# Repeated multiplications of a constant matrix on TensorE, in six places of a four-layer convolution kernel

## The reference, cut to what matters

```python
x = x + _L0_conv_ref(_gn(x), ...)   # 1x1 conv, norm, SiLU, 6 gated radial bases, 1x1 conv, norm, SiLU
x = x + _L1_conv_ref(_gn(x), ...)   # projection, depthwise 3x3 conv, SiLU, linear attention, layer norm, projection
x = x + _L2_conv_ref(_gn(x), ...)   # attention over the 256 places, 8 heads
x = x + _L3_conv_ref(_gn(x), ...)   # deformable 3x3 conv
```

```python
zxbcdt = jnp.einsum('bhwc,oc->bhwo', x, W_in)
xBC = jax.nn.silu(depthwise 3x3 conv of xBC + conv_b)
KV = jnp.einsum('bln,blhd->bhnd', Bm, V_scaled)
y = jnp.einsum('bln,bhnd->blhd', Cm, KV) + xs * D[None, None, :, None]
y = y * jax.nn.silu(z)
y = (y - mu) * jax.lax.rsqrt(var + 1e-05) * ln_g + ln_b
out = jnp.einsum('bld,od->blo', y, W_out)
```

## Time and profile before

| | us |
|---|---|
| median of 3 runs | 539.01 (535.24 to 540.68) |
| profiled execution | 540.11 |
| span of its trace | 538.3 |
| TensorE busy | 421.3 (78%) |
| DVE busy | 342.4 (64%) |
| ACT busy | 295.2 (55%) |

### The profile page before, as it was taken

The page is one execution under the profiler, slowest core; times in us unless marked ns, Lnnn a source line. Parts: engine busy times, 40 slices in busy tenths (PEclk is TensorE's granted clock), DMA queues, the critical chain, the costliest instruction groups (busy, mean ns, idle before and its releaser), DMA issues. The chain is left out here.

```text
span 538.3 us, 9045 instructions
## 1 busy us (share of the span) xinstructions
PE 421.3 (78%) x3242; PEld 211.8 (39%) x3242; DVE 342.4 (64%) x668; ACT 295.2 (55%) x515; POOL 132.9 (25%) x162
## 2 busy tenths in 40 slices
PE   1415672399999863858999999965977999999995
PEld 1213551245554432512333333333533545455442
DVE  4437787403334537897999999434365878788784
ACT  1359993105145413705888888852675668486441
POOL 4420002200000000665442211104063618155000
PEclk9855997579999956865999999995999999999999
DMA  5500000530000000493220000006464290743302
GB/s 139 160 0 1 0 0 0 119 76 0 1 1 0 1 0 0 127 311 113 82 80 2 4 2 2 2 1 148 99 188 101 58 208 2 185 80 64 70 2 78
DMA packets 20765, 33.77 MB, mean 63 GB/s; under 512 B 5656, under 2 KB 15496, under 8 KB 19956
## 3 DMA queue, kind: packets, MB, share of 16 engines
q1 hardware_dynamic: 16724, 23.70, 18.2%
q0 software_dynamic: 2176, 6.35, 4.3%
q10 hardware_dynamic: 1824, 3.19, 2.2%
HBM read 16.21 MB, written 4.64 MB: 39 GB/s over the span
## 5 line engine op out<-in xcount | busy, mean ns | idle before, releaser
L1308 DVE TENSOR_TENSOR L_s<-L_row_ps,L_cols 128x1024 f32<-128x1024 f32 x72 | 87.7, 1219 | 7.1 <-PE L_row_ps L1473 6.5
L884 DVE TENSOR_REDUCE L_mx<-L_ring 128x2 f32<-128x512 f32 x128 | 83.3, 687 | 10.9 <-PE L_ring L1007 10.3
L939 ACT ACTIVATE L_e<-L_ring 128x512 f32<-128x512 f32 x128 | 73.8, 598 | 20.8 <-PE L_ring L1020 18.8
L1496 PE MATMUL L_acc<-L_s,L_t_sb 128*64 128x256 f32 x576 | 78.0, 392 | 1.4 <-DVE L_s L1308 1.2
L1377 ACT ACTIVATE L_cols<-L_col_ps 128x512 f32<-128x512 f32 x72 | 42.9, 597 | 47.4 <-PE L_col_ps L1483 47.0
L1007 PE MATMUL L_ring<-stacks_k_st,stacks_q_st 64*128 64x256 bf16 x256 | 50.8, 301 | 6.3 <-DVE L_v_all L873 4.6
L1496 PEld LDWEIGHTS L_acc<-L_s,L_t_sb 128*64 128x64 f32 x576 | 34.9, 136 | 34.3 <-DVE L_s L1308 20.7
L1020 PE MATMUL L_ring<-stacks_q_st,stacks_k_st 64*128 64x256 bf16 x256 | 47.1, 281 | 1.3 <-DMA stacks_q_st<-L_m_parts 1.3
L1473 PE MATMUL L_row_ps<-L_hats,L_sel 48*128 48x512 bf16 x144 | 43.2, 381 | 0.0
L1040 PE MATMUL L_ctx_ps<-L_e,L_v_x 128*32 128x256 f32 x512 | 41.1, 395 | 0.0
L370 PE MATMUL L_y<-L_t,all_w_post 128*128 128x256 f32 x96 | 25.1, 416 | 14.3 <-DVE L_t L330 14.3
(11 more groups left out here) (267 smaller groups left out, 788.0 us busy)
## 6 DMA issues: line engine op xcount, KB each, us to landing
L_hats<-L_parts SPq DMA_DIRECT2D x28, 216.0 KB, 4.9
L_hat<-L_offsets SPq DMA_DIRECT2D x20, 192.0 KB, 4.7
L_mask<-L_offsets SPq DMA_DIRECT2D x10, 192.0 KB, 5.1
stacks_q_st<-L_q_parts SPq DMA_DIRECT2D x12, 128.0 KB, 3.9
stacks_k_st<-L_k_parts ACTq DMA_DIRECT2D x12, 128.0 KB, 4.8
stacks_q_st<-L_q_parts POOLq DMA_DIRECT2D x12, 128.0 KB, 2.7
stacks_k_st<-L_k_parts POOLq DMA_DIRECT2D x12, 128.0 KB, 2.9
L_stack<-L_xpad SPq DMA_DIRECT2D x7, 162.0 KB, 5.9
```

The costliest lines, as they stand in the source:

```text
L884: dve.tensor_reduce(mx[:, n % 2, :, head], ring[:, place(step) % 3].rearrange("p (q s) -> p q s", q=2), AX.X, ALU.max).then_inc(max_read, 1)
L939: act.activation(e[:, k], ring[:, 3 + v % 3], ACT.Exp, scale=HD2 ** -0.5).then_inc(e_ready, 1)
L1308: dve.tensor_tensor(s[:, q], row_ps[:, q], cols[:, t % 3:t % 3 + 1].broadcast_to([P, 2, 2 * N]), ALU.mult).then_inc(s_ready, 1)
L1496: mm = pe.matmul(acc[C * e:C * e + C, b, 0:N], t_sb[:, b, h, (KK * e + t) * C:(KK * e + t + 1) * C], s[:, q, h, e * N:(e + 1) * N], start= ...
```

## The change

A new function `keep_clock` issues a number of multiplications of `avg2` by itself, each 128 by 128 with 128 columns moving, into a part of PSUM that is free at that moment. Nothing reads the products, and they signal nothing. It is called in six places: behind the last norm of layer 0 (20 multiplications); in layer 1 behind the norm (17), ahead of the four groups (4), in the last quad's three waits (5, 3 and 9) and behind the last quad (20); in layer 2 behind the norm (4). That is 82 in all.

```diff
+def keep_clock(pe, avg2, out, count):
+    for _ in range(count):
+        pe.matmul(out[:, 0:P], avg2[:], avg2[:], start=True, stop=True)
...
                 gn_2.tensor(pe)
+                keep_clock(pe, avg2, y1[:, 6], 20)
...
                 gn.tensor(pe)
                 weights.wait(pe, 1)
+                keep_clock(pe, avg2, xs_ps[:, 0], 17)
                 pe.wait_ge(g_ready, 1)
...
                     if more:
                         conv_xs(q + 1, 0, 2)
+                    else:
+                        keep_clock(pe, avg2, xs_ps[:, 0], 5)
...
                         conv_xs(q + 1, 2, 4)
+                    else:
+                        keep_clock(pe, avg2, xs_ps[:, 0], 3)
...
                         conv_xs(q + 1, 4, 8)
+                    else:
+                        keep_clock(pe, avg2, xs_ps[:, 0], 9)
...
+                keep_clock(pe, avg2, xs_ps[:, 0], 4)
                 for g in range(NQ):
                     pe.wait_ge(stack_in[g], 64)
...
                 quad(NQ - 1, False)
+                keep_clock(pe, avg2, xs_ps[:, 0], 20)
...
                 weights.wait(pe, 2)
+                keep_clock(pe, avg2, ring[:, 5], 4)
```

## The result

The changed kernel took 534.23 us (median of 20 runs, 530.47 to 536.67) against 538.76 for the kernel before in the same session (20 runs, 534.32 to 543.33), 0.84% less by the medians; the ratio is 0.9944, 95% interval 0.9921 to 0.9966. So it is faster, by 0.56 to 0.84%, which is within the 1% that the prediction called no change, and 2.9 us above the 531.3 that was forecast. All sessions taken together, this one included, 145 runs of before have a mean of 537.99 us and 52 of after 533.84: minus 4.15, with a standard error of 0.32, or 0.77%. The runs of after also lie closer together: standard deviation 1.6 us against 2.8. Means here take in all runs, since on this one core their spread is the thing to be explained.

What follows compares the result with a forecast made beforehand. TensorE, the busiest engine, was taken to hold others up at clock 0.50 in two stretches. 540.11 - 4.1 (convolution) - 4.57 (last quad) + 0.4 (layer 1's end) - 0.5 (layer 2) = 531.3 us; 8-in-10 range 528 to 537.

Steps and rivals of the forecast that it cites:

- the two stretches: Layer 1's convolution groups and last quad, where TensorE worked at clock 0.50 while others waited; gains of 4.41 and 4.57 us.
- the sum: Whole kernel: 540.11 - 4.1 - 4.57 + 0.4 - 0.5 = 531.3 us, from the profiled execution, taken as the median.
- it shifts: Layers 2 and 3 hang on layer 1's end by waits, so they move earlier as a whole.
- Step 1: Price of one added multiplication: 0.24 us at full clock, 0.45 at half.
- Step 2: Layer 0's end: the 20 multiplications take about 6.4 us of 7.8 available, no cost; bound plus 1.2.
- Step 3: Ahead of the convolution: 17 and 4 multiplications cost plus 0.2 us, plus 3.0 if all at half clock.
- Step 4: Convolution's four groups at full clock: minus 4.41 us; net of the multiplications ahead and transfer waits minus 4.1.
- Step 5: Layer 1's last quad at full clock: minus 4.57 us; the 5, 3 and 9 multiplications fit their waits.
- Step 6: End of layer 1: the 20 multiplications end some 0.4 us after DVE, plus 0.4, between 0 and plus 4.6.
- Step 7: Start of layer 2: four multiplications fit; first projection pair about 1.0 us faster, given half: minus 0.5.
- only one of the two stretches pays: Rival: the clock gaps are not filled to the end, so only one stretch gains; 536 us, chance 0.17.
- Given back: Rival: the won time is lost at the blocks' ends and the transfers; 537.5 us, chance 0.08.

Runs made afterwards that it cites:

- more_places_2: Second run of the whole change plus 19 multiplications at the start, 10 instead of 4 at layer 2, 9 around its end, 19 at layer 3's start: 527.05 us, ratio 0.9805.
- after_3: The changed kernel run again without an edit, for a third trace: 533.61 us, ratio 0.9963 against the kernel before.
- after_4: The changed kernel run again without an edit, for a fourth trace: 533.64 us, ratio 0.9946 against the kernel before.
- more_places: The whole change plus 19 multiplications at the start, 10 instead of 4 at layer 2, 9 around its end, 19 at layer 3's start: 526.40 us, ratio 0.9779.
- after_less: The changed kernel without the 20 multiplications behind layer 1 and the 4 ahead of layer 2's projections: 533.10 us, ratio 0.9903 against the kernel before.

## Why the prediction was wrong

The mechanism of the two stretches was right, the size of what the change wins was not: 8.8 us in the prediction (540.11 to 531.3), 4.15 in the means. **The step that failed is the sum**, in two of its statements. At "I take the sum as it stands for the median" it takes the two stretches of one profiled execution for those of every execution: the traces have w_q 6.7 us earlier, 0.5 of it in the norm ahead of it, where steps 3 to 6 add up to 8.3. At "it shifts" it puts the answer of layers 2 and 3 at nothing: they took 1.75 us more. That the time spread by 5.4 us was seen there, and put down in part to where the clock rises; what should have followed is that the profiled execution, dear in both stretches, has more to give than the median.

- Step 1 (0.24 and 0.45 each) held: 1.28 us for 5, 0.94 for 3, 2.17 for 9, and 0.215 for each further one; at half clock, in more_places_2, 3.62 for 8.
- Step 2 held: 6.34 us against 6.4, ended ahead of DVE (6.04 to 6.34 in the four traces).
- Step 3 held: 5.67 us for the 17 against 5.6, but 6.89 and 6.87 in after_3 and after_4, where TensorE came to the product that needs w_g (L638) at 102.77 and 103.22, the latter past the 103 that was named as a sign of a wrong step, and the first group no longer waited for its transfer. In the profile shown the convolution began at 104.31 instead of 104.85, as the transfer came 0.47 us earlier than in the profile of before; that is no gain of the change.
- Step 4: right in the pair of profiles (17.57 to 13.18, and no wait between groups), mis-sized for the median. Eight traces with nothing ahead of the convolution have 15.25 to 17.69, mean 16.47. The gain is 3.3, not 4.4; by the times of the kernels without layers 2 and 3 it is 2.4 (0.9).
- Step 5: the same. Eight traces without the quad's multiplications have 14.28 to 17.35, mean 16.04: the gain is 3.2, not 4.57; by the times 4.0 (1.0). The three waits held what was put into them, as predicted.
- Step 6: plus 0.21 instead of 0.4.
- Step 7 was too small. The norm ahead of the projections ran at the higher clock, and from L167 to w_q it took 3.34 us instead of 3.85, which the step did not have. The first pair was at half clock in two traces (0.55 as shown; L995 2.08 us) and at full clock in two, as the half chance had it; the projections gained 1.4 in the mean.
- "It shifts" failed: from the first w_q on after took 1.75 us more in the mean of four traces each. Behind the gain of the projections that is a loss of some 3.2: 1.35 in layer 3's stage, where the clock falls behind a longer pause, nearly all the rest in layer 2. Why the pause is longer, and what slows layer 2, stays open.

The sum with these sizes: -3.3 - 3.2 + 0.2 - 0.5 = -6.8, and the four traces of each kernel have w_q 6.7 us earlier (210.4 to 203.7); plus 1.75 given back is -5.0, and the mean spans differ by 4.9 (536.5 to 531.6). The times say -4.15 (0.32). That last 0.8 lies within what four traces of a kernel can tell.

Of the rivals, "only one of the two stretches pays" came closest in time (536), for a reason that the runs refute: both pay, each less. "Given back" named layer 0's end, the groups and layer 1's end; none of them gave back more than 0.2 us. The places were layers 2 and 3, which no rival named. The chance of "faster" is also mis-added: nine tenths of 0.70 are 0.63, so it comes to 0.67 and not 0.71.

The prediction followed its rows (1.7%) against the under 1% of the Trainium skill's "TensorE: Matmul & The Clock Gate", Part 1; this change's 0.77% is under that figure. The more_places kernel, 2.0 to 2.2% faster than before, is not: so it is no bound for this kernel. The same section of the Trainium skill warns that such a start is run-variable, with a different number of slow matmuls from one run to the next; the 15.5 beside 17.6 us in the table agree. That variation is what the sum had left out.

## What to carry to other kernels

Where a gain hangs on the granted clock, one profile is one draw: take several executions of the kernel before, and size the gain by the mean of the stretch, not by the one that is shown. Fill a wait with no more than it holds (one multiplication too many costs 0.215 us each here), and fill every wait ahead of work that is on the path: one half of the change fixed its own stretch and nothing else. And measure the stages behind the gain too: an engine that comes earlier to a wait which ends where it ended before wins nothing there, and the longer pause can let the clock fall for the products behind it (3.22 us instead of 1.91 here).

## What the runs showed of the hardware

The same stretch, with the same waits ahead of it, took 15.25 to 17.69 us in eight traces, as the clock rose earlier or later in it. They are not spread evenly: four took 15.25 to 15.56 us, four 17.34 to 17.69. With multiplications ahead of it the stretch took 13.17 or 13.18 in all the traces that have them. One wait of 1.68 us in layer 3 was followed by a clock of 0.52 (404.40 to 406.40 in after), one of 0.84 us at the same place by 1.00 (406.20 to 408.20 in after_less). And the same four full-width multiplications ahead of layer 2's projections were followed by a clock of 0.55 and 0.50 over the next 3.2 us in two traces of after and by 1.00 in the other two; the two traces with ten have the first product at 1.12 and 1.11 us, and all that have none there 2.04 us or more.
